# Layer 0 of a four-layer graph kernel: a mask moved partly from TensorE to VectorE, totals turned in 32x32 blocks, and sums taken two heads at a time

## The reference, cut to what matters

```
q, k, vv = x1 * SCALE, x2, v          # each split into 8 heads of 32
scores = einsum('hnd,hmd->hnm', q, k)
scores = where(adj > 0, scores, -9e15)
attn   = softmax(scores, axis=-1)
out    = einsum('hnm,hmd->hnd', attn, vv)
x      = layernorm(x + out)
```

## Time and profile before

| | |
|---|---|
| median of three runs | 873.53 us |
| the profiled execution: time, span | 873.28 us, 871.6 us |
| mean granted TensorE clock | 0.983 |
| layer 0 | 0 to 406.2 us of the span |
| TensorE busy, whole span | 93% |
| VectorE, ScalarE busy, whole span | 79%, 67% |
| from 300 to 340 us | TensorE 39.76, VectorE 36.52, ScalarE 29.88 us of 40 |

### The profile page before, as it was taken

One profiled execution on the slowest core, in us unless ns is written; L12 is line 12 of the kernel. 1 busy time (PEld: TensorE's weight loads), 2 busy tenths in 40 slices (PEclk: granted clock), 3 DMA queues, 4 the chain that ended last, 5 costly groups with the idle time before them and its releaser, 6 DMA issues. The chain is left out here.

```text
span 871.6 us, 18880 instructions
## 1 busy us (share of the span) xinstructions
PE 814.6 (93%) x7820; PEld 510.7 (59%) x7820; DVE 688.7 (79%) x1045; ACT 581.2 (67%) x608; POOL 149.4 (17%) x287
## 2 busy tenths in 40 slices
PE   3999999999999999995869999999988999999997
PEld 1344444344444444442559999999944557777786
DVE  7587979898998989896889999999853595555454
ACT  6798989896777767671479999999959731111000
POOL 3501012653110100000520000000001352111122
PEclk9999999999999999997979999999998999999999
DMA  8965354393211010002121110011000000000011
GB/s 292 263 196 165 110 149 131 109 242 88 84 25 49 13 49 1 13 1 66 42 100 52 52 40 30 34 51 52 3 1 1 1 1 1 1 1 1 2 49 49
DMA packets 28183, 56.85 MB, mean 65 GB/s; under 512 B 5760, under 2 KB 9984, under 8 KB 26560
## 3 DMA queue, kind: packets, MB, share of 16 engines
q1 hardware_dynamic: 23968, 46.19, 17.2%
q0 software_dynamic: 4128, 9.44, 4.1%
HBM read 38.70 MB, written 2.23 MB: 47 GB/s over the span
## 5 line engine op out<-in xcount | busy, mean ns | idle before, releaser
L484 ACT ACTIVATE ex<-scores_ps,shift 128x1024 f32<-128x1024 f32 x256 | 262.5, 1130 | 77.3 <-PE scores_ps L344 69.4
L555 DVE TENSOR_TENSOR esum<-esum,ex 128x1024 f32<-128x1024 f32 x192 | 223.0, 1212 | 6.1 <-ACT ex L484 6.1
L340 PE MATMUL scores_ps<-qst,kst 128*128 128x512 f32 x512 | 201.6, 475 | 2.5 <-ACT ex L484 1.8
L994 PE MATMUL banks<-fx,pos 128*128 128x132 f16 x2048 | 161.7, 223 | 9.4 <-DVE fx L1097 5.4
L1262 ACT ACTIVATE steps<-a_all,big_b_head 128x2048 fp8e5<-128x2048 f32 x87 | 166.2, 1988 | 0.0
L344 PE MATMUL scores_ps<-edge,negI 128*128 128x512 fp8e5 x512 | 155.3, 385 | 0.0
L340 PEld LDWEIGHTS scores_ps<-qst,kst 128*128 128x128 f32 x512 | 90.2, 189 | 69.6 <-ACT ex L484 18.2
L994 PEld LDWEIGHTS banks<-fx,pos 128*128 128x128 fp8e5 x2048 | 122.2, 98 | 11.5 <-issue 8.4
L1001 PE MATMUL banks<-fm,edge 128*128 128x66 f16 x2048 | 104.8, 194 | 0.0
L1001 PEld LDWEIGHTS banks<-fm,edge 128*128 128x128 fp8e5 x2048 | 87.3, 98 | 0.0
L1166 DVE TENSOR_TENSOR pos<-steps,edge 128x1024 int32<-128x1024 int32 (+1 forms) x65 | 76.9, 1203 | 11.1 <-PE banks L994 5.5
(11 more groups left out here) (209 smaller groups left out, 933.4 us busy)
## 6 DMA issues: line engine op xcount, KB each, us to landing
adj_raw<-in_adjT_dram SPq DMA_DIRECT2D x32, 512.0 KB, 5.2
a_all<-score_rows_dram SPq DMA_DIRECT2D x8, 1024.0 KB, 4.6
kst<-high_low SPq DMA_DIRECT2D x56, 64.0 KB, 4.5
kst<-high_low POOLq DMA_DIRECT2D x56, 64.0 KB, 4.9
qst<-high_low POOLq DMA_DIRECT2D x56, 64.0 KB, 2.2
qst<-high_low SPq DMA_DIRECT2D x56, 64.0 KB, 3.6
ex<-in_x2T_dram SPq DMA_DIRECT2D x2, 1024.0 KB, 6.8
ex<-in_xT_dram SPq DMA_DIRECT2D x2, 1024.0 KB, 8.8
```

Of the source, the lines that this page charges most:

```text
L340: nc.tensor.matmul(to, kst[:, h, jt * P:(jt + 1) * P], qst[:, it % 2, h, :], start=True, stop=False)
L484: nc.scalar.activation(ex[:, s % ER, h, :], scores_ps[:, u % SR, :], ACT.Exp, bias=shift[:, it // NC * HG + h:it // NC * HG + h + 1], scal ...
L555: nc.vector.tensor_tensor(esum[:, h, :], other, ex[:, s % ER, h, :], ALU.add).then_inc(summed, 1)
L994: done = nc.tensor.matmul(place(half, i), pos[:, group_of(h, k, half) % GR, jt % GU, i * P:(i + 1) * P], fx[:, e, jt].rearrange("p k r c - ...
```

## The change

- **Masks.** `VEILED = {0: 3, 2: 1, 4: 1, 6: 1}`: in step 0 the units of the first three heads, and in steps 2, 4 and 6 that of the first head, are left without their two mask matmuls. VectorE multiplies the unit's exponentials with (edge == 0) in place, by a `scalar_tensor_tensor` of 128 x 1024 (`veil`), before it adds them. The mix of such a step waits for it. That is six units a round, 48 in all.
- **Sums.** `add(s, h, count)`: one addition for two heads, 128 x 2048, after every second unit; only the last step of all keeps single ones.
- **Closing.** `keep` becomes `close`: the totals are turned by VectorE in 32x32 blocks, the 16 distinct columns get floor, minimum and reciprocal, and are turned back with each repeated 32 times. Its pieces stand in steps 1 and 2.
- **Copy.** `mixed_ps` goes to `yT` on ScalarE (`keep_mixed`), after the fourth Exp of step 0, and waits there for the mixes.

```diff
+    VEILED = {0: 3, 2: 1, 4: 1, 6: 1}
...
-                        nc.tensor.matmul(to, kst[:, h, jt * P:(jt + 1) * P], qst[:, it % 2, h, :], start=True, stop=False)
-                    for t in range(2):
+                        last = nc.tensor.matmul(to, kst[:, h, jt * P:(jt + 1) * P], qst[:, it % 2, h, :], start=True, stop=bare)
+                    for t in range(0 if bare else 2):
...
                     pe.wait_ge(exp_ready, HG * (s + 1))
+                    if jp in VEILED:
+                        pe.wait_ge(veiled, veils_to(s))
...
+                def keep_mixed(it):
+                    act.wait_ge(mixed, (it + 1) * JP)
+                    nc.scalar.copy(yT[:, it // NC, columns(it % NC)], mixed_ps).then_inc(stored, 1)
...
+                        if jp == 0 and it and h == HG - 1:
+                            keep_mixed(it - 1)
...
+                def add(s, h, count):
+                    it, jp, hh = s // JP, s % JP, slice(h, h + count)
+                    dve.wait_ge(exp_ready, s * HG + h + count)
...
+                    nc.vector.tensor_tensor(esum[:, hh, :], other, ex[:, s % ER, hh, :], ALU.add).then_inc(summed, count)
+
+                def veil(s, h):
+                    it, jp = s // JP, s % JP
+                    dve.wait_ge(exp_ready, s * HG + h + 1)
+                    at = ex[:, s % ER, h, :].rearrange("p (t n) -> p t n", t=2)
+                    nc.vector.scalar_tensor_tensor(out=at, in0=edge[:, 2 * jp:2 * jp + 2, columns(it % NC)], scalar=0.0,
+                                                   in1=at, op0=ALU.is_equal, op1=ALU.mult).then_inc(veiled, 1)
...
+                def close(it, piece):
+                    g, at, done = it // NC, columns(it % NC), it * CLOSING
                     if piece == 0:
-                        dve.wait_ge(mixed, (it + 1) * JP)
-                        nc.vector.tensor_copy(yT[:, g, at], mixed_ps).then_inc(stored, 1)
+                        dve.wait_ge(totals, it + 1)
+                        nc.vector.transpose(turned, total_ps).then_inc(recip_step, 1)
                     elif piece == 1:
-                        dve.wait_ge(totals, it + 1)
-                        nc.vector.tensor_scalar(recip, total_ps, TRUST / 2, None, ALU.max).then_inc(recip_step, 1)
-                    elif piece == 2:
-                        dve.wait_ge(recip_step, it * (PIECES + 1) + 1)
-                        nc.vector.tensor_reduce(out=least[:], in_=recip, axis=AX.X, op=ALU.min).then_inc(lowest, 1)
+                        dve.wait_ge(recip_step, done + 1)
+                        nc.vector.tensor_scalar(compact[:], turned.rearrange("p (b r) -> p b r", r=DH)[:, :, 0], TRUST / 2, None,
+                                                ALU.max).then_inc(recip_step, 1)
+                        dve.wait_ge(recip_step, done + 2)
+                        nc.vector.tensor_reduce(out=least[:], in_=compact[:], axis=AX.X, op=ALU.min).then_inc(lowest, 1)
                         dve.wait_ge(lowest, it * 2 + 1)
                         nc.vector.tensor_tensor(low, least[:], low, ALU.min).then_inc(lowest, 1)
-                        dve.wait_ge(lowest, it * 2 + 2)
-                    elif piece < 3 + PIECES:
-                        part = slice((piece - 3) * CW // PIECES, (piece - 2) * CW // PIECES)
-                        nc.vector.reciprocal(recip[:, part], recip[:, part]).then_inc(recip_step, 1)
+                        nc.vector.reciprocal(compact[:], compact[:]).then_inc(recip_step, 1)
+                    elif piece == 2:
+                        dve.wait_ge(recip_step, done + 3)
+                        nc.vector.transpose(recip, compact[:].unsqueeze(2).broadcast_to([P, CW // DH, DH])).then_inc(recip_step, 1)
...
                     for h in range(HG):
-                        if jp:
-                            add(s, h)
-                        elif it:
+                        if h < VEILED.get(jp, 0):
+                            veil(s, h)
+                        if s == STEPS - 1:
+                            add(s, h, 1)
+                        elif jp and h % 2:
+                            add(s, h - 1, 2)
+                        elif it and not jp:
                             halve(it - 1, h)
```

More of the change, by code:

```diff
@@ L109, in attention @@
     QUADS = {"k": ((0, 2), (1, 3)), "q": ((0, 1), (2, 3))}
-    PIECES = 4
+    CLOSING = 4
+    VEILED = {0: 3, 2: 1, 4: 1, 6: 1}
     ER = 3
@@ L139, in attention @@
         esum = S.sb("esum", [P, HG, 2 * CW], fp32)
-        recip, res = half_sum[:, 0, :], half_sum[:, 1, :]
+        recip, res, turned = half_sum[:, 0, :], half_sum[:, 1, :], half_sum[:, 2, :]
         spare = adj_raw[:].rearrange("p a t n -> p (a t n)").bitcast(fp32)
@@ L144, in attention @@
         least = S.sb("least_sum", [P, 1], fp32)
+        compact = S.sb("distinct_sums", [P, CW // DH], fp32)
         parts = S.sb("high_low", [P, HL, 2, CW], fp32r)
@@ L199, in adds_before, with veils_to @@
             return it * ADDS + (jp - 1) * HG + h + 1
+        def veils_to(s):
+            it, jp = s // JP, s % JP
+            return it * sum(VEILED.values()) + sum(VEILED[v] for v in VEILED if v <= jp)
         with nc.Block() as block:
@@ L326, in score @@
                     it, jp, u = s // JP, s % JP, s * HG + h
-                    g = it // NC
+                    g, bare = it // NC, h < VEILED.get(jp, 0)
                     if h == 0:
@@ L383, in sum_weights @@
                     pe.wait_ge(wa_step, 4 * KT)
-                    pe.wait_ge(recip_step, (s // JP - 1) * (PIECES + 1) + 1)
+                    pe.wait_ge(recip_step, (s // JP - 1) * CLOSING + 1)
                     for k in range(KT):
@@ L497, in _ @@
                             convert(s + AHEAD + 1)
+                keep_mixed(ROUNDS - 1)
             @block.vector
@@ L543, in _ @@
                 nc.vector.tensor_copy(shift[:], pair_ps[:, 0, 0:H]).then_inc(shift_kept, 1)
-                def add(s, h):
+                def add(s, h, count):
+                    it, jp, hh = s // JP, s % JP, slice(h, h + count)
+                    dve.wait_ge(exp_ready, s * HG + h + count)
+                    if h == 0:
+                        dve.wait_ge(veiled, veils_to(s))
+                    if jp == 1:
+                        if it:
+                            dve.wait_ge(halved, (it - 1) * HG + h + count)
+                        other = ex[:, (s - 1) % ER, hh, :]
+                    else:
+                        dve.wait_ge(summed, adds_before(it, jp - 1, h + count - 1))
+                        other = esum[:, hh, :]
+                    nc.vector.tensor_tensor(esum[:, hh, :], other, ex[:, s % ER, hh, :], ALU.add).then_inc(summed, count)
+                def veil(s, h):
                     it, jp = s // JP, s % JP
                     dve.wait_ge(exp_ready, s * HG + h + 1)
[L548 to L555, removed]
+                    at = ex[:, s % ER, h, :].rearrange("p (t n) -> p t n", t=2)
+                    nc.vector.scalar_tensor_tensor(out=at, in0=edge[:, 2 * jp:2 * jp + 2, columns(it % NC)], scalar=0.0,
+                                                   in1=at, op0=ALU.is_equal, op1=ALU.mult).then_inc(veiled, 1)
                 def halve(it, h):
@@ L562, in halve @@
                                             ).then_inc(halved, 1)
-                def keep(it, piece):
-                    g, at = it // NC, columns(it % NC)
-                    step = Chain(dve, recip_step, it * (PIECES + 1))
+                def close(it, piece):
+                    g, at, done = it // NC, columns(it % NC), it * CLOSING
                     if piece == 0:
-                        dve.wait_ge(mixed, (it + 1) * JP)
-                        nc.vector.tensor_copy(yT[:, g, at], mixed_ps).then_inc(stored, 1)
+                        dve.wait_ge(totals, it + 1)
+                        nc.vector.transpose(turned, total_ps).then_inc(recip_step, 1)
@@ L627, in flip @@
                     dve.wait_ge(scores_ready, HG * JP * (NC + c + 1))
+                    dve.wait_ge(veiled, sum(VEILED.values()) * (NC + c + 1))
                     marks = edge[:, tt, columns(c)].bitcast(int32)
@@ L640, in _ @@
                         piece = (jp - 1) * HG + h
-                        if it and 0 <= piece <= 4 + PIECES:
-                            keep(it - 1, piece)
+                        if it and 0 <= piece <= CLOSING:
+                            close(it - 1, piece)
                         if W_AT + 2 <= s < W_AT + 4:
@@ L652, in _ @@
                             flip(it - NC - 1, (jp - 4) * 2 + h // 2)
-                for piece in range(5 + PIECES):
-                    keep(ROUNDS - 1, piece)
-                    if piece == 2:
+                for piece in range(CLOSING + 1):
+                    close(ROUNDS - 1, piece)
+                    if piece == 1:
+                        dve.wait_ge(lowest, ROUNDS * 2)
                         nc.vector.tensor_scalar(fine[:], low, TRUST, None, ALU.is_ge).then_inc(fine_made, 1)
```

(2 more changed lines are left out.)

8 lines of the change are left out of this document (4 added, 4 removed).

## The result

The changed kernel takes 902.93 us, median of four runs (900.51 to 905.47), against 873.70 for the kernel before: a ratio of 1.0327 [1.0308, 1.0346], 3.3% slower. The profiled execution took 900.51 (span 898.8), the fastest of the four, so what the trace explains is 27.2 us of span; the medians lie 29.2 apart. The mean granted clock is 0.976 (0.983 before).

The account below looks back on a forecast made before the run. Two rings were taken as the bound, ScalarE with TensorE per pair of steps and VectorE per round, the latter ending last. 873.3 + 16.8 (rounds +19.7, end -2.9) + 5.6 for the clock = 895.7 us; range 888 to 904.

Parts of the forecast that it names:

- the end: End of layer 0, after the last total: 3.65 us instead of 6.54, all on the path, so -2.9 us.
- The masks on TensorE, worth nothing: Units losing their masks on TensorE stand outside the ring: gain taken as 0, at most 0.1 us a pair, 2.8 us.
- the ring: Pair of steps: odd step's first unit, five Exps, even step's fourth unit, mixes, first unit again; TensorE alone 0.1 us faster.
- TensorE is the bound: Rival: each unit without mask returns 0.46 us on TensorE, 48 times 22, giving 849 us with the end; chance 5%.
- The veils, 1.14 each: VectorE's six veils a round cost 1.14 us each, like an addition: 6.84 us a round.
- the rival of cheap veils: Rival: veils on VectorE run at two elements a cycle, 0.52 us less each, giving 871 to 874 us; chance 6%.
- The sums, -1.0 a round, +1.02 for the second Exp: VectorE's merged additions save 0.07 x 14 = 1.0 us a round; step 1's first pair needs two Exps, +1.02.
- The closing, -3.95: VectorE's closing with 32x32 turnings, copy hidden on ScalarE: 2.55 us left of 6.5, so 3.95 saved a round.
- dear: Rival: a turning at 3.44 us gives 921 us, or veils at 2.28 each add 6.8 a round, 943; chance 7%.
- The sum of a round, +2.9 (early +2.7), 19.7 in all: VectorE's terms add 2.9 us a round, early rounds 2.7 by ScalarE's ring: 3 x 2.7 + 4 x 2.9 = +19.7.
- The three veils before the halvings are what TensorE waits for: At each hand-over between rounds, TensorE's total starts some 3 us late because of these veils.
- The clock, 7 x 0.8 = 5.6: TensorE's waits of 3.2 to 3.4 us make the clock fall at most hand-overs: 0.8 us each, +5.6.

Follow-up runs that it names:

- Experiment 5: Changed kernel, halvings before veils, three veils a round: third unit of steps 0 and 2, second of step 1; 870.00 us, ratio 0.9955.
- experiment 4: Changed kernel, halvings before veils, three veils a round: fourth unit of steps 0 and 2, first of step 1; 863.34 us, ratio 0.9880.
- experiment 3: Changed kernel with `VEILED` empty, all masks back on TensorE; new sums, closing and copy kept; 867.65 us, ratio 0.9930.
- experiment 2: Changed kernel with the four halvings moved ahead of the three veils in step 0, same instructions; 872.82 us, ratio 0.9991.
- experiment 8: Changed kernel with one addition for each head again, 28 a round instead of 14; 904.48 us, ratio 1.0350.
- Experiment 1: Changed kernel with twelve overwritten matmuls on TensorE before the wait for the halvings, in six of seven hand-overs; 895.38 us, ratio 1.0246.
- experiment 6: Changed kernel, halvings before veils, eight veils a round: fourth unit of even steps, first of odd steps; 916.08 us, ratio 1.0475.
- experiment 7: Kernel before the change with only the six veils a round added; single additions, old closing, copy on VectorE; 934.38 us, ratio 1.0702.

## Why the prediction was right, and the two terms that were too small

895.7 was forecast and 902.93 measured, within the range and in the mechanism of the forecast. Against the profiled execution, 900.51, it is 4.8 short: the rounds +5.4, with what follows the seventh hand-over, the end +0.2, the rest of the program -0.9.

- *The masks on TensorE, worth nothing.* Right. Experiment 5 takes masks off neighbours of the ring and its pairs stay at 11.09; experiment 4 takes as many off the ring and gets 6.7 us. And with all masks back on TensorE (experiment 3) the kernel is faster than with the six units' off it (experiment 2). The rival "TensorE is the bound" fell with it, 99% busy or not.
- *The veils, 1.14 each.* Right: 1219 ns long, 1.14 from start to start, as an fp32 addition of that size, though one input is fp8. With that the rival of cheap veils is gone.
- *The sums, -1.0 a round, +1.02 for the second Exp.* The first addition does wait for the second Exp (339.41 against 337.21). That both about cancel agrees with experiment 8.
- *The closing, -3.95.* The turnings are 0.72 and 0.71 long, and the second takes 0.64 from start to start, where I took 0.60, so they aren't dear. I took the copy as hidden; that holds in the changed kernel, but in rounds 1 to 3 only because its hand-overs are long (experiment 3). At the end of the layer it is 3.87 against 3.65, 2.7 us saved instead of 2.9.
- *The sum of a round, +2.9 (early +2.7), 19.7 in all.* 2.5 us too small. Experiment 1 has hand-overs without a fall: 2.8 twice, then 3.3 four times. With 3.3 for the one that wasn't filled, that sums to 22.2. The third was priced as an early one and cost what the later ones do, 0.6 more. For the others, what I left out is in the row of L572: additions waited 2.4 us in all right behind a veil on the same tile, 0.20 at a time, once or twice a round. From start to start such a veil is 0.28 longer.
- *The three veils before the halvings are what TensorE waits for.* Right: experiment 2 moves them behind and the 30 us are gone. The other veils, and these in their new place, still take the 6 us that sums, closing and copy give.
- *The clock, 7 x 0.8 = 5.6.* 3 us too small, or more: of the 30.7 us by the last run of Exps (420.75 against 390.01), 0.2 arose before the rounds and 22.2 are hand-overs without a fall; 8.3 is left for the falls, and the medians lie another 2 us further apart. There were five falls, not seven, and experiment 1 makes each worth 1.6 to 1.9 us, not 0.8. I had counted how much longer the total and the first units could take at half clock, 2.8, and cut that to under a third, in case the fall came in the gap. At four of the five it came with the total: the rows at 333.42 and 337.21 have 0.87 more for the total and 0.71 for what follows up to the Exp, 1.58 at that hand-over. At the last one the total was nearly done (1.21 long) and the units behind it paid.

The gain that the change could have had went into the wait it made. Take the veils out and it is 0.7% faster; put three of them into the ring behind the halvings and it is 1.2% faster than before.

## What to carry to other kernels

Work that fills an engine's idle time has to stand behind what the other engine waits for: the same veils cost 30 us more ahead of the halvings than behind them, and behind them still 5. Before moving work off an engine that is 99% busy, find the ring that spaces its stages and take the work from a member of it; three units inside gave 6.7 us more than three beside it. And a new wait of TensorE can cost more than its length: look at the matmuls behind it, and price a fall of the clock by all that lies on the path there.

## What the runs showed of the hardware

- In layer 0 the clock didn't fall at totals that had waited 1.69 (experiment 6), 1.71 (7 and 8) and 2.63 us (the changed kernel, twice), and did at those that had waited 2.71 (8), 3.13, 3.50 and up to 7.59. But in layer 2 it fell after 2.01, so the length of the wait alone doesn't decide. Twelve overwritten bf16 matmuls in the gap, 2.76 us, kept it at 1.00.
- A fall lasted 3.4, 6.8 or 10.2 us. The two of 10.2 are in experiment 7, at totals that had waited 7.59 and 6.53; one that had waited 7.42 had 6.8.
- A veil with fp8 and fp32 inputs runs like an fp32 addition, 1219 ns for 1024 columns. A 128x512 turning in 32x32 blocks takes 717 ns out of PSUM and 712 when its source is 16 columns, each read 32 times.
- ScalarE copies 128x512 fp32 out of PSUM in 0.58 us.
